# Last layer of a four-layer kernel: routing inside the attention block, early weight loads, scatter and gather without a pace

## The reference

```python
def _L3_attn_ref(x, ln_g, ln_b, W_in, b_in, W_out, b_out, gamma_q, beta_q, gamma_k, beta_k):
    ...
    xn = (x - mu) * jax.lax.rsqrt(var + LN_EPS) * ln_g + ln_b
    uvz = jax.nn.silu(jnp.einsum('bld,df->blf', xn, W_in) + b_in)
    u, v, z = (uvz[..., :E], uvz[..., E:2 * E], uvz[..., 2 * E:])
    q = z * gamma_q + beta_q
    k = z * gamma_k + beta_k
    attn = jnp.einsum('bqs,bks->bqk', q, k) / seq_len
    attn = jnp.square(jax.nn.relu(attn))
    out = u * jnp.einsum('bqk,bke->bqe', attn, v)
    return x + jnp.einsum('ble,ed->bld', out, W_out) + b_out

def _L3_ffn_ref(x, wg, w1, b1, w2, b2):
    ...
    combine, dispatch = _top1_gate(tokens, wg, capacity)
    dispatched = jnp.einsum('sec,sm->ecm', dispatch, tokens)
    h = jax.nn.relu(jnp.einsum('ecm,emf->ecf', dispatched, w1) + b1[:, None, :])
    expert_out = jnp.einsum('ecf,efm->ecm', h, w2) + b2[:, None, :]
    combined = jnp.einsum('sec,ecm->sm', combine, expert_out)
    ...
    xn = _layernorm(x, axis=-1)
    x = x + _L3_attn_ref(xn, ...) + _L3_ffn_ref(xn, ...)
```

## Time and profile before

| what | value |
|---|---|
| median of 3 runs | 2017.84 us (2017.4 to 2018.54) |
| the profiled execution | 2014.04 us, its span 2012.1 us |
| TensorE, VectorE, ScalarE, GpSimd busy | 78%, 67%, 52%, 40% of the span |
| last layer | norm from 1735.75 us, routing from 1767.89, attention and experts from 1781.15 |

### The profile page before, as it was taken

How to read it: one execution, slowest core, us unless ns; L and a number is a source line. 1 busy time by engine, 2 the same in 40 slices (tenths; PEclk the granted TensorE clock), 3 DMA queues, 4 the chain that set the end, 5 groups by cost and what they waited for, 6 DMA issues and landing times. The chain is left out here.

```text
span 2012.1 us, 35698 instructions
## 1 busy us (share of the span) xinstructions
PE 1563.5 (78%) x12141; PEld 1070.2 (53%) x12143; DVE 1340.9 (67%) x2371; ACT 1045.9 (52%) x1858; POOL 799.5 (40%) x803
## 2 busy tenths in 40 slices
PE   5986887887866567457788889994589999649994
PEld 5753665665644444425566666662245444437883
DVE  7537777787899998685433348868762699436334
ACT  1468778787754454144333336664354577434440
POOL 1575556555688885276011124331500000024005
PEclk9997999999987888578899999997689999769997
DMA  5211111110010010565311115522651242111322
GB/s 149 93 62 51 55 45 34 50 50 29 19 31 25 24 24 9 214 201 106 55 43 44 43 39 91 87 40 70 131 86 55 38 66 37 54 51 40 100 69 78
DMA packets 153319, 130.35 MB, mean 65 GB/s; under 512 B 18929, under 2 KB 137864, under 8 KB 152914
## 3 DMA queue, kind: packets, MB, share of 16 engines
q1 hardware_dynamic: 140626, 104.57, 21.1%
q0 software_dynamic: 12544, 23.82, 4.5%
HBM read 77.08 MB, written 52.43 MB: 64 GB/s over the span
## 5 line engine op out<-in xcount | busy, mean ns | idle before, releaser
L662 POOL TENSOR_TENSOR xn_t<-xn_t,scan_du 128x512 f32<-128x512 f32 x256 | 321.5, 1270 | 179.0 <-ACT xn_t L804 101.3
L707 PE MATMUL banks<-scan_hc,ident 128*128 128x256 f32 x1024 | 297.4, 417 | 73.7 <-DVE scan_hc L859 73.5
L853 DVE TENSOR_TENSOR_SCAN xn_t<-banks,xn_t 128x512 f32<-128x512 f32 x256 | 311.5, 1217 | 41.3 <-ACT banks L794 35.0
L2272 ACT ACTIVATE att_pr<-banks 128x768 f32<-128x768 f32 (+1 forms) x256 | 234.3, 916 | 139.2 <-PE banks L2164 80.3
L794 ACT ACTIVATE banks<-delta,scan_exp_centre,a_neg 128x255 f32<-128x255 f32 x512 | 265.2, 559 | 47.3 <-DVE xn_t L853 47.0
L707 PEld LDWEIGHTS banks<-scan_hc,ident 128*128 128x128 f32 x1024 | 194.1, 208 | 136.2 <-DVE scan_hc L859 101.7
L859 DVE TENSOR_TENSOR scan_hc<-xn_t,banks 128x512 f32<-128x512 f32 x256 | 175.8, 687 | 28.1 <-PE banks L692 16.1
L2317 DVE TENSOR_REDUCE att_mb<-banks 128x4 f32<-128x1024 f32 x128 | 154.0, 1222 | 25.0 <-PE banks L2131 20.2
L913 POOL DMA_INDIRECT disp<-xn_tok,places x128 | 135.3, 1057 | 86.0 <-issue 61.2
L2180 PE MATMUL banks<-att_pr,att_vx 128*32 128x256 f32 (+1 forms) x2048 | 155.0, 376 | 4.9 <-ACT att_ot L2277 3.5
L2313 DVE TENSOR_REDUCE att_mb<-banks 128x6 f32<-128x768 f32 x128 | 121.6, 956 | 40.1 <-PE banks L2138 38.2
(11 more groups left out here) (342 smaller groups left out, 3348.1 us busy)
## 6 DMA issues: line engine op xcount, KB each, us to landing
scan_ew<-f_packed SPq DMA_DIRECT2D x12, 578.0 KB, 4.2
q_parts<-att_p_parts SPq DMA_DIRECT2D x16, 384.0 KB, 4.1
k_parts<-att_p_parts SPq DMA_DIRECT2D x16, 384.0 KB, 6.0
att_qs<-q_parts SPq DMA_DIRECT2D x64, 96.0 KB
att_ks<-k_parts SPq DMA_DIRECT2D x64, 96.0 KB
gau_ew<-f_packed SPq DMA_DIRECT2D x8, 578.0 KB, 4.1
disp<-zeros SPq DMA_DIRECT2D x1, 4608.0 KB, 15.9
att_xin<-disp SPq DMA_DIRECT2D x72, 64.0 KB, 1.8
```

Source lines behind the costliest of these rows:

```text
L662: nc.gpsimd.tensor_tensor(bu[:, i % RING], b_sb[:, q % 2], du[:, b % 2, c:c + 1, :].to_broadcast([P, 2, T]), ALU.mult).then_inc(s.bu_made, 1)
L707: ins = nc.tensor.matmul(bank(Y_BANK)[:, c, :], g.ident[:], hc[:, i % RING, n, :], start=False, stop=(i % (PAIRS * DC) == PAIRS * DC - 1 a ...
L853: v.tensor_tensor_scan(rows(h[:, i % 2]), g.ps[:, DA + i % RING, :], rows(bu[:, i % RING]), 0.0, ALU.mult, ALU.add).then_inc(s.scan_done, 1)
L2272: nc.scalar.activation(pr[:, i % RING], g.ps[:, at:at + 2, 0:W], ACT.Exp, scale=scale).then_inc(s.p_ready, 1)
```

## The change

Routing loses its section. Its jobs run inside the attention block, on each engine at a place written by hand: on VectorE choice first and place behind the first q, k and v bias; the Exp on ScalarE behind two scaled batches; the two counting matmuls behind the first v projection. The nine weight tensors and two experts' weights are loaded in the norm, ahead of the zero fill. The second factor is computed in the norm (`second=r`, without a row of weights). Scatters wait for the places alone and gathers for the stored results alone; `paced` is gone. The experts begin three steps earlier, and the steps of `combine` follow.

```diff
 def normalise(..., prefetch=None, second=None):
+        second_row = second is not None and second.row is not None
+        if second_row:
+            wr = s.sb("norm_row", [P, D])
         if second:
-            wr = s.sb("norm_row", [P, D])
             var2 = s.sb("var2", [P, NT])
...
-                if second:
+                if second_row:
                     sp.dma_start(wr[:], second.row).then_inc(s.row_in, 16)
...
                     second_root(nc, dve, s.r2_step, s.r2_sqrt, var2, std2, inv2, second.r2)
+                if second_row:
                     dve.wait_ge(s.row_in, 16)
...
                     nc.scalar.activation(std2[:], var2[:], ACT.Sqrt).then_inc(s.r2_sqrt, 1)
+                if second and not second_row:
+                    nc.scalar.preload_act_table(ACT.Exp)
 def routing(...):
     def vector(dve):
+        vector_choice(dve)
+        vector_place(dve)
...
         dve.sem_inc(s.r_chosen, 1)
+        choice_steps = c.n
+
+    def vector_place(dve):
+        c = Chain(dve, s.r_step, choice_steps)
+        v = nc.vector
         dve.wait_ge(s.r_pos, 1)
 def layer3(nc, g, t, out):
-        normalise(nc, g, "norm3", g.x, g.xn, g.xn_t, router=t["f3_gate"], n_exp=E3, disp=disp)
-        route(nc, g, t, "route3", E3, 1, CAP3, 0, r)
+        r.r2 = c.enter_context(nc.sbuf_tensor("factor3", [P, NT], F32))
+        r.row = None
         gated_and_experts(nc, g, t, out, disp, ybuf, r)
 def gated_and_experts(nc, g, t, out, disp, ybuf, r):
-    FIRST = 29
-    AHEAD = 6
+    FIRST = 26
...
+        def weights(sp):
+            for dst, src in ((ln_g, t["a3_g"]), (ln_b, t["a3_b"]), (w, t["a3_w"]), (bu, t["a3_bu"]),
+                             (bz, t["a3_bz"]), (bv, t["a3_bv"].to_broadcast([P, EG])), (qk, t["a3_qk"]),
+                             (wo, t["a3_wo"]), (bo, t["a3_bo"].to_broadcast([P, D]))):
+                sp.dma_start(dst[:], src).then_inc(s.w_in, 16)
+            for e in range(2):
+                sp.dma_start(ew[:, e], t["f3_packed"][e]).then_inc(ew_in[e], 16)
+
+        normalise(nc, g, "norm3", g.x, g.xn, g.xn_t, router=t["f3_gate"], n_exp=E3, disp=disp, prefetch=weights, second=r)
+        job = routing(nc, g, s, s.sb, t, "route3", E3, 1, CAP3, 0, r, banks=(H_BANK, TY_BANK))
+        r2 = r.r2
...
         def combine_step(j):
-            return max(Q_GATHER + GRP * (j + 1) + 6, 4 * (GRP * (j + 1) // QT) + 1)
+            return max(Q_GATHER + 3 * (j + 1) + 6, 4 * (GRP * (j + 1) // QT) + 1)
...
             def _(sp):
-                for dst, src in ((ln_g, t["a3_g"]), (ln_b, t["a3_b"]), (w, t["a3_w"]), (bu, t["a3_bu"]),
...
-                    sp.dma_start(dst[:], src).then_inc(s.w_in, 16)
...
-                load_weights(0)
-                load_weights(1)
                 sp.wait_ge(s.scattered, NT * 16)
...
             def _(pool):
+                job.gpsimd(pool)
+                pool.wait_ge(s.r_placed, 1)
                 for i in range(NT):
-                    if i >= AHEAD:
-                        pool.wait_ge(s.paced, i - AHEAD + 1)
                     pool.indirect_dma_start(disp, bass.IndirectOffsetOnAxis(ap=r.scat_i[:, 0, i:i + 1], axis=0),
...
                 for i in range(NT):
-                    pool.wait_ge(s.paced, min(Q_GATHER + i + 1, STEPS))
                     pool.indirect_dma_start(gb[:, i, :], None, ybuf,
...
                 project_uz(0)
                 project_v(0)
+                job.tensor(pe)
                 for step in range(STEPS):
...
-                    pe.sem_inc(s.paced, 1)
...
             def _(act):
-                act.wait_ge(s.r2_step, 3)
-                nc.scalar.activation(std[:], var[:], ACT.Sqrt).then_inc(s.r2_sqrt, 1)
-                nc.scalar.preload_act_table(ACT.Silu)
-                act.wait_ge(s.w_in, 144)
-                act.wait_ge(s.r2_step, 8)
-
...
                 scaled_rows(0)
                 scaled_rows(1)
+                act.wait_ge(s.w_in, 144)
+                job.scalar(act)
+                nc.scalar.preload_act_table(ACT.Silu)
+                take_turned(0)
                 scaled_rows(2)
-                for b in range(3):
-                    take_turned(b)
+                take_turned(1)
+                take_turned(2)
                 scaled_rows(3)
...
                 vv = nc.vector
-                second_factor(nc, g, dve, s.r2_step, s.r2_sqrt, var, std, inv, r2)
                 dve.wait_ge(s.w_in, 144)
...
+                job.vector_choice(dve)
                 make_qk(0)
                 bias_v(0)
+                job.vector_place(dve)
                 for step in range(STEPS):
```

More of the change, by code:

```diff
@@ L982, in vector, with vector_choice @@
     def vector(dve):
+        vector_choice(dve)
+        vector_place(dve)
+    choice_steps = 0
+    def vector_choice(dve):
+        nonlocal choice_steps
         c = Chain(dve, s.r_step)
@@ L1111, in routing @@
     job.sync, job.tensor, job.scalar, job.vector, job.gpsimd = sync, tensor, scalar, vector, gpsimd
+    job.vector_choice, job.vector_place = vector_choice, vector_place
     return job
@@ L1375, in gated_and_experts @@
     names = [f"gathered{j}" for j in range(NGRP)]
-    with section(nc, "gau", *names, "w_in", "rows_in", "r2_step", "r2_sqrt", "xs_ready", "turned", "xt_ready",
+    with section(nc, "gau", *ROUTE, *names, "w_in", "xs_ready", "turned", "xt_ready",
                  "z_ready", "u_ready", "v_ready", "z_done", "u_done", "v_done", "vb_done", "scaled", "qk_ready",
-                 "s_ready", "relu_done", "a_ready", "o_ready", "g_ready", "f_ready", "f_taken", "x_step", "paced", "scattered",
+                 "s_ready", "relu_done", "a_ready", "o_ready", "g_ready", "f_ready", "f_taken", "x_step", "scattered",
                  "ex_in0", "ex_in1", "ew_in0", "ew_in1", "e_turned", "ext_ready", "h_ready", "act_done", "y_ready",
@@ L1389, in gated_and_experts @@
         ln_b = s.sb("ln_b", [P, 1])
-        var = s.sb("var", [P, NT])
-        std = s.sb("std", [P, NT])
-        inv = s.sb("inv", [P, NT])
-        r2 = s.sb("r2", [P, NT])
+        ew = s.sb("ew", [P, 2, WN])
+        ex_in, ew_in, stored = (s.ex_in0, s.ex_in1), (s.ew_in0, s.ew_in1), (s.stored0, s.stored1)
+        def weights(sp):
[8 more added lines that the diff above has]
+        r2 = r.r2
         xs = s.sb("xs", [P, 4, QT, D])
@@ L1404, in gated_and_experts @@
         gt = s.sb("gt", [P, EC, T])
-        ew = s.sb("ew", [P, 2, WN])
         exin = s.sb("exin", [P, 2, CT, D])
@@ L1410, in gated_and_experts @@
         gb = s.sb("gb", [P, NT, D])
-        gathered = s.sems[:NGRP]
-        ex_in, ew_in, stored = (s.ex_in0, s.ex_in1), (s.ew_in0, s.ew_in1), (s.stored0, s.stored1)
+        gathered = s.sems[len(ROUTE):len(ROUTE) + NGRP]
         def chunk_rows(c):
@@ L1428, in _ @@
             def _(sp):
-                for dst, src in ((ln_g, t["a3_g"]), (ln_b, t["a3_b"]), (w, t["a3_w"]), (bu, t["a3_bu"]),
-                                 (bz, t["a3_bz"]), (bv, t["a3_bv"].to_broadcast([P, EG])), (qk, t["a3_qk"]),
-                                 (wo, t["a3_wo"]), (bo, t["a3_bo"].to_broadcast([P, D]))):
-                    sp.dma_start(dst[:], src).then_inc(s.w_in, 16)
                 def load_weights(e):
-                    if e >= 2:
-                        sp.wait_ge(s.y_out, 2 * e - 2)
+                    sp.wait_ge(s.y_out, 2 * e - 2)
                     sp.dma_start(ew[:, e % 2], t["f3_packed"][e]).then_inc(ew_in[e % 2], 16)
```

## The result

| | before | changed | ratio, 95% interval |
|---|---|---|---|
| first comparison, 4 and 4 runs | 2017.62 us (2015.63 to 2018.54) | 1986.11 us (1985.47 to 1988.78) | 0.9866 [0.9847, 0.9885] |
| second, 7 and 4 runs (run f1) | 2012.14 us (2010.33 to 2017.62) | 1986.72 us (1985.66 to 1988.14) | 0.9868 [0.9851, 0.9885] |
| third, 13 and 4 runs (run e4) | 2131.82 us (2127.51 to 2139.96) | 2160.08 us (2158.75 to 2164.12) | 1.0126 [1.0099, 1.0153] |

The third row has the other sign. It belongs to a condition of the machine that the first traces did not show; I call it the lag.

What follows compares the result with a forecast made beforehand. The end was taken to be set by when GpSimd's last gathers may begin and how fast they issue. The terms 16.7 - 1.7 - 1.8 + 6.7 = 19.9 us, off 2017.84, gave 1997.9 us, range 1992.0 to 2004.0.

Steps and rivals of the forecast that it cites:

- step 5: Unpaced scatters: 31 intervals cost 42.3 us with VectorE collisions, 39.5 without; tokens 16.7 us earlier, TensorE waiting 3.5 to 5.
- step 7: TensorE's clock ahead of the experts: idling drops it to 1.2 GHz for a while, costing 1.8 us.
- steps 1 and 2: Norm and routing section: second factor adds 0.67 us, table load and delayed fill nothing; the removed section gives 13.26 us.
- steps 3 and 4: Attention block's start: V bias at t0 + 12.05, places at t0 + 17.0, first attend about t0 + 17.9; first scatter 1786.5.
- t0: Start of the last layer's attention block, forecast at 1768.56 us after the routing section's removal.
- rival B: Scatters and gathers: no interference and so less waiting, scatters 39.5 us, gathers 1.30 throughout; 1992.9 us, chance 0.15.
- rival C: TensorE ahead of the experts: the clock holds despite the idle, saving 1.8 us; 1996.1 us, chance 0.12.
- step 6: Expert steps 25 to 42 instead of 28 to 45: eight more matmuls ahead of the gathers, +1.7 us, 2.5 at most.
- step 8: Gather train: last expert result to last gather 45.1 us against 51.8, because pace held it back; 6.7 us gained.
- Rival A: Scatters and gathers: VectorE's port fully blocks the unpaced trains, intervals 1.90 us; 2024 us, slower, chance 0.04.

Runs made afterwards that it cites:

- f1: The changed kernel run again, nothing else altered, without the lag; 1986.72 us, ratio 0.9868 against the kernel before.
- e4: The changed kernel run once more, nothing else altered, with the lag; 2160.08 us, ratio 1.0126 against the kernel before.
- g4: The changed kernel with its eleven weight loads issued at the attention block's start instead of in the norm, with the lag; 2181.22 us, ratio 1.0199.
- h1: The changed kernel with FIRST 29 and a fixed GpSimd memset ahead of each last-layer scatter and gather, without the lag; 2009.28 us, ratio 1.0009.
- f2: The changed kernel with the pace back on the scatters alone and FIRST 29, without the lag; 1989.02 us, ratio 0.9889.
- i2: The changed kernel with both paces back, FIRST 29 and the placing ahead of the first scaled queries, with the lag; 2120.38 us, ratio 0.9936.
- h2: The changed kernel with both paces back, FIRST 29 and the placing ahead of the first scaled queries, without the lag; 1988.16 us, ratio 0.9906.

## Why the prediction was right and wrong

The direction and the mechanism were right, the size was not, and two things made it wrong. The first is in the layer, in steps 5 and 7: the collisions of the unpaced scatters and the dip of the clock were charged too high, by 3.9 us together. The second is a term that the sum put at nothing: everything outside the last layer. Against the profiled execution, from norm start on: tokens 18.8 us earlier (forecast 16.7), the experts' stretch +1.3 (+3.5), last result to last gather -7.6 (-6.7), tail 0. 18.8 - 1.3 + 7.6 = 25.1 us, forecast 19.9. With 25.1 alone the median would have come to 1992.7, just inside the range; the other 6 us took it out.

1. Norm (steps 1 and 2): right. Block start 12.57 us earlier relative to the norm (forecast 12.59), table load free, zero fill hidden.
2. Side job (steps 3 and 4): right to 0.1 us. First attend t0 + 18.01 (17.9), first scatter t0 + 17.99 (17.94). g4 bears out the weights' part.
3. Scatter without pace, step 5: **this is where the sum failed.** I charged two collisions of together 0.47 us to every attention cycle, read from a pair in the paced train. The unpaced one meets VectorE's SBUF stretch less regularly: 40.5 us for 31 intervals, 42.3 forecast, 39.5 for none. The last scatter was undisturbed as well, so the way to the tokens took 5.31 and not 5.66 us. Together 2.1 us. For the scatters rival B, no interference, was the nearer one: 39.5 against 40.5 measured.
4. The clock, step 7, fell with it. TensorE reached step 25 when I said (1827.74; forecast 1829.5 to 1831 less the 3.2 us by which this block starts earlier), but the tokens came 2.1 us sooner than forecast, so the idle was 1.43 us and not 3.5 to 5. The 1.8 us for a dip never arose, and in this rival C, the clock holds, came true, but because the wait was short, not because the clock held behind a long one. The mechanism was right where the idle was long: 4.08 us ahead of the attention's first batch cost 1.7 us of work (mean clock 0.67 over 5.17 us), and h1's 7.9 us cost 1.4.
5. The expert steps, step 6: +1.3 us, +1.7 forecast. f2 shows it (101.8 with FIRST 29, 103.1 with 26).
6. Gathers, step 8: 44.2 us from last result to last gather, 45.1 forecast. Again the collisions were overcharged: the train took 41.5 us, 42.5 forecast, 40.3 for none. Attention's last add starts 7.1 us ahead of the last gather, so it doesn't bind.
7. Rival A, full blocking: it did not come. The last layer's scatters lose 1.0 us in all to collisions. In the front layers single scatters are blocked as it says: besides, one of 4.04 us beside a 4.42 us addition in the first layer, and of 1.68 and 2.01 us beside additions of 1.22 us in the second. Why instructions of 0.41 to 0.69 us held the last layer's scatters so little stays open.
8. What no term held: that the pace might protect TensorE. In the condition with the lag the changed kernel is 28 us slower, ratio 1.0126. The side job and the early weights still gain 7.6 us there, while the part that the trace seemed to price most simply, taking away two waits, loses 37.8. No row of the trace of before told of it, and a chance of 0.04 for slower left no room for it. The sign of the forecast therefore held only in the condition in which it was made, and that the first comparison met this condition was luck.
9. The level: 6.4 of the 31.5 us lie outside the last layer. 3.2 of them are the norm's start in the two profiles (1735.8 before, 1732.6 changed), and most of the rest is that the median before lay 3.6 us above its profiled execution and the changed one's 0.6 above its own. Both are spread: without the lag the norm starts anywhere from 1730.1 to 1740.6, and the medians of before are 2006.63 to 2017.62. I had taken the difference from the trace alone and called 4 us the measurement's grain. With its own before in the second comparison the median is 25.4 us lower, which is the layer's gain.

## What to carry to other kernels

Measure a change of one stage from the start of that stage, in several profiles: here the front moved by more than most terms. A wait that looks like pure delay may keep two engines from disturbing each other; before taking it away, try the kernel in more than one session. Where a row of DMAs is long, a short gap may have to stay: 0.7 us between two instructions was enough here. It has a price: without the lag the fixed gaps cost 26 us against the changed kernel (h1 against f1), the two old paces 4.8 and 7.4. And a collision rate that was read from a train paced by attention's steps doesn't hold for the same train without the pace.

## What the runs showed of the hardware

- Beside an unbroken row of indirect GpSimd DMAs (one per 1.27 us) TensorE can fall to one matmul per 2.80 us, and what it hands to VectorE and ScalarE comes 9 to 16 us late (e4), while the DMA instructions keep their pace. The Trainium skill, page "SBUF — State Buffer", section "Who interferes with whom", says that PE and ACT never wait on anyone; of the SBUF ports no run contradicts that, but a PE that seems free of all others was not free here. It shows in some sessions and not in others, and every execution here was recorded by the profiler.
- A gap of 0.7 us between the DMA instructions removes it in the last layer (276.6 us with the lag, 276.9 without); a pace that lets 13 scatters through in a row leaves 7.3 us of it (i2 against h2).
- An indirect DMA of 128 rows takes GpSimd 0.97 (scatter) or 1.00 us (gather) and 0.30 us to the next; scatters land 2.2 us, gathers 2.6 us after issue.
- After 7.9 us of idleness TensorE ran 2.8 us at 1.2 GHz (h1), and after 4.08 us its mean clock over the next 5.17 us was 0.67; after 1.4 us it ran on at 2.4 GHz.
- Scatters beside long VectorE additions of two SBUF operands ended 0.84 to 0.94 us behind the addition's end: 4.04 and 4.77 us beside additions of 4.4 us, 1.68 and 2.01 us beside 1.22. In the last layer, beside instructions of 0.41 to 0.69 us, the held ones took 1.07 to 1.49 us, and most took 0.97.
